# Subtracting the running maxima on TensorE in the hgt passes of a graph-network kernel

## What is computed

```
a = (kw * q_e).sum(-1) * pri[:, etype].T / sqrt(D)      # one score per edge and head
amax = segment_max(a, dst)
ea = exp(a - amax[dst])
att = ea / segment_sum(ea, dst)[dst]
h = segment_sum(m * att[:, :, None], dst)
```

## Time and profile before

| | before |
|---|---|
| median of 3 runs | 7814.15 us (7812.76 to 7823.77) |
| the profiled execution's own time | 7818.18 us |
| span of the profiled execution | 7816.4 us |
| first hgt pass, from its first load to its last add | 5353.4 to 6094.7 us |
| second hgt pass, to its last add | up to 7110.7 us |
| busy over the span | PE 66%, DVE 63%, POOL 46%, ACT 34% |

### The profile page before, as it was taken

How to read it: one execution, slowest core, us unless ns; L and a number is a source line. 1 busy time by engine, 2 the same in 40 slices (tenths; PEclk the granted TensorE clock), 3 DMA queues, 4 the chain that set the end, 5 groups by cost and what they waited for, 6 DMA issues and landing times. The chain is left out here.

```text
span 7816.4 us, 109527 instructions
## 1 busy us (share of the span) xinstructions
PE 5146.3 (66%) x21617; PEld 3624.5 (46%) x21618; DVE 4929.8 (63%) x12062; ACT 2667.4 (34%) x6461; POOL 3569.9 (46%) x3776
## 2 busy tenths in 40 slices
PE   4762667567746956676756664876777767776764
PEld 4762334334424834556733344853444444444443
DVE  6875677767766157543366665157999549996453
ACT  2551455144511210002213311224777137772321
POOL 1774677067700257760147710234666026661014
PEclk9999777777778987787856776999999899998777
DMA  2541444144411943335624411965777137772036
GB/s 83 163 145 53 116 126 125 22 120 125 125 17 49 314 121 87 88 82 212 215 78 107 106 22 31 321 192 173 211 211 208 34 124 212 210 211 72 21 98 199
DMA packets 516240, 1021.81 MB, mean 131 GB/s; under 512 B 135829, under 2 KB 276930, under 8 KB 507278
## 3 DMA queue, kind: packets, MB, share of 16 engines
q0 software_dynamic: 191360, 489.21, 23.3%
q1 hardware_dynamic: 294095, 497.29, 19.7%
q10 hardware_dynamic: 30528, 32.52, 1.2%
HBM read 928.22 MB, written 90.27 MB: 130 GB/s over the span
## 5 line engine op out<-in xcount | busy, mean ns | idle before, releaser
L731 POOL DMA_INDIRECT l_hgt_ep_g<-l_tkm,l_hgt_ep_ix x832 | 924.3, 1111 | 439.5 <-PE l_hgt_ep_out L816 235.9
L731 POOL DMA_INDIRECT l_gat_ep_g<-l_gat_th,l_gat_ep_ix x832 | 844.5, 1015 | 240.1 <-issue 232.4
L816 PE MATMUL l_gat_ep_out<-l_gat_ep_g,l_gat_ep_here 128*126 128x264 f32 x1664 | 686.0, 554 | 160.9 <-DVE l_gat_acc L965 152.4
L816 PEld LDWEIGHTS l_gat_ep_out<-l_gat_ep_g,l_gat_ep_here 128*126 128x126 f32 x1664 | 376.8, 256 | 382.5 <-DVE l_gat_acc L965 310.9
L2315 DVE TENSOR_TENSOR f_moe_experts_yb<-f_moe_experts_py,f_moe_experts_b2s 128x256 f32<-128x256 f32 x208 | 88.4, 425 | 719.3 <-PE f_moe_experts_py L2298 700.9
L2266 POOL DMA_INDIRECT f_moe_experts_xg<-f_moe_tx,f_moe_tok x208 | 196.4, 944 | 743.2 <-PE f_moe_experts_px L2279 626.8
L816 PE MATMUL l_hgt_ep_out<-l_hgt_ep_g,l_hgt_ep_here 128*126 128x288 f32 x1664 | 500.2, 424 | 53.5 <-DVE l_hgt_ep_g L951 52.2
L855 ACT COPY l_gat_ep_stage<-l_gat_ep_out 30x264 f32<-30x264 f32 x832 | 308.7, 372 | 563.2 <-PE l_gat_ep_out L816 551.5
L2486 POOL DMA_INDIRECT l_edges_g<-l_table,l_edges_ix x416 | 413.8, 995 | 179.9 <-issue 100.2
L2330 ACT ACTIVATE f_moe_experts_ht<-f_moe_experts_phid,f_moe_experts_b1b 128x128 f32<-128x128 f32 x848 | 242.0, 372 | 734.6 <-PE f_moe_experts_phid L2289 730.1
L524 POOL DMA_INDIRECT recs<-place_stage,place_pos x392 | 425.0, 1084 | 138.5 <-issue 117.4
(11 more groups left out here) (603 smaller groups left out, 11877.5 us busy)
## 6 DMA issues: line engine op xcount, KB each, us to landing
l_hgt_ep_hot<-locrow SPq DMA_DIRECT2D x208, 256.0 KB, 4.9
f_moe_experts_w1b<-in_L_ffn_w SPq DMA_DIRECT2D x32, 1024.0 KB, 6.8
f_moe_experts_w2b<-in_L_ffn_w SPq DMA_DIRECT2D x32, 1024.0 KB, 7.6
f_moe_experts_w1b<-in_L_ffn_w SPq DMA_DIRECT2D x64, 512.0 KB
f_moe_experts_w2b<-in_L_ffn_w SPq DMA_DIRECT2D x64, 512.0 KB
f_moe_experts_w1b<-in_L_ffn_W SPq DMA_DIRECT2D x56, 512.0 KB, 4.8
f_moe_experts_w2b<-in_L_ffn_W SPq DMA_DIRECT2D x56, 512.0 KB, 4.9
l_gat_ep_hot<-locrow SPq DMA_DIRECT2D x104, 256.0 KB
```

The costliest lines, as they stand in the source:

```text
L731: gp.indirect_dma_start(g[:, b % NB, j, 0:W], None, table, bass.IndirectOffsetOnAxis(ap=ix[:, b, j:j + 1].bitcast(U32), axis=0)).then_inc( ...
L816: pe.matmul(out[:, t % 4, 0:WO], here[:, b % 2, t, :], g[:, b, t, F:F + WO], start=True, stop=True).then_inc(s_out, 1)
```

## The change

In "hgt" passes alone, `x` and `less` go. TensorE's `turn_back` becomes `less_top`: a matmul of `raw` with the identity starts a sum in PSUM and a second one, of `top` with a new constant `minus` (minus the identity), adds to it, so that PSUM holds raw less maximum, in two buffers by parity of the step. ScalarE's `exponent` becomes `keep_top`: it takes the exponent straight from PSUM, and then copies the two columns of `top` to `refs`. On VectorE the backward scan follows the forward one at once, and the adds 1, 2 and 3 follow it one after the other. `scan` waits for ScalarE's copy of two steps before (`s_refs`, one more semaphore for each edge pass of any kind) in place of `s_back`, and `score` no longer waits for `s_x`. GpSimd makes `minus` at the start.

```diff
+            gp.affine_select(out=core.minus[:, :], in_=core.ones[:, :], compare_op=ALU.is_equal, fill=0.0,
+                             base=0, pattern=[[1, 128]], channel_multiplier=-1).then_inc(made, 1)
+            gp.wait_ge(made, 5)
+            gp.tensor_scalar(core.minus[:, :], core.minus[:, :], -1.0, None, ALU.mult)
...
-        x = ph.sb("x", [128, 2, CT, H])
+        x = ph.sb("x", [128, 2, CT, H]) if kind != "hgt" else None
...
+        apart = back[:, 0:2 * R].rearrange("p (b t h) -> p b t h", b=2, h=H) if kind == "hgt" else None
...
+        s_refs = ph.sem("refs")
...
+            def less_top(k, b):
+                if later(k):
+                    pe.wait_ge(s_ex, k - 1)
+                pe.matmul(back[:, b % 2 * R:b % 2 * R + R], core.ident[:, :], raw[:, b % 2, :, :].rearrange("p t h -> p (t h)"),
+                          start=True, stop=False, skip_group_check=True)
+                pe.wait_ge(s_top, k + 1)
+                pe.nop(nofuse=True)
+                pe.matmul(back[:, b % 2 * R:b % 2 * R + R], top[:, b % 2, :], core.minus[0:R, 0:R],
+                          start=False, stop=True, skip_group_check=True).then_inc(s_back, 1)
...
-                piped(pe, NCH, [(2, total(0)), (0, whose), (1, turn), (2, total(1)), (1, turn_back), (0, queries)], NB)
+                piped(pe, NCH, [(2, total(0)), (0, whose), (1, turn), (2, total(1)), (1, less_top), (0, queries)], NB)
...
+            def keep_top(k, b):
+                act.wait_ge(s_back, k + 1)
+                act.activation(g[:, b, :, X:X + H], apart[:, b % 2, :, :], ACT.Exp).then_inc(s_ex, 1)
+                act.copy(refs[:, :, bass.ds(k, 1)].rearrange("r s o -> r (s o)"), top[:, b % 2, 0:128:127]).then_inc(s_refs, 1)
...
-                piped(act, NCH, [(3, take(0)), (3, take(1)), (2, exponent), (0, one_hot), (1, rows_here)], NB)
+                piped(act, NCH, [(3, take(0)), (3, take(1)), (2, keep_top), (0, one_hot), (1, rows_here)], NB)
...
                     v.wait_ge(s_back, k - 1)
-                    v.wait_ge(s_x, k - 1)
+                    if kind != "hgt":
+                        v.wait_ge(s_x, k - 1)
...
-                    v.wait_ge(s_back, k - 1)
+                    v.wait_ge(s_refs if kind == "hgt" else s_back, k - 1)
...
-                piped(v, NCH, [now(score), add(0), now(scan), add(1), now(scan_back), add(2), now(less), add(3), now(weigh(0))], NB)
+                piped(v, NCH, [now(score), add(0), now(scan), now(scan_back), add(1), add(2), add(3), now(weigh(0))], NB)
```

More of the change, by code:

```diff
@@ L116, in constants @@
     core.low = keep.sb("low", [128, 128])
+    core.minus = keep.sb("minus", [128, 128])
     core.iota = keep.sb("iota", [128, 128])
```

## The result

The changed kernel takes 7797.32 us (median of 14 runs, 7787.74 to 7829.2), the kernel before beside it 7816.05 (14 runs, 7801.73 to 7831.4): ratio 0.9979, 95% interval 0.997 to 0.9987, 16 us less by the ratio and 19 by the medians. That is faster, as forecast, but about half of the 34 us (35 less, 1 more) that the sum had taken off. The profiled execution took 7805.18 us, span 7803.4.

A forecast was written before the change was run, and what follows sets the result against it. Two equally long chains, VectorE's queue and TensorE's loop through scans and queries, were taken to bound the step. Step 6.78 to 6.61, 0.17 x 208 = 35 us less, 1 more: 7818.2 to 7784, median 4 lower, 7780; range 7762 to 7825.

The forecast's parts named there:

- the 34 us (35 less, 1 more): Whole kernel: 0.17 x 208 = 35 us less from the steps, 1 us more for semaphores and GpSimd's constant.
- Undisturbed step 6.61: VectorE's queue in an hgt step: mean step 6.78 before, 6.61 after.
- The 0.40 that goes is paid back but for 0.03: VectorE: two instructions holding 0.40 go, but three adds standing together, each waiting for the last, take back all but 0.03.
- TensorE's loop 6.56: TensorE: queries at 4.44, next key multiplication possible 2.12 later, at 6.56, 0.05 shorter than VectorE's 6.61.
- L900 overlaps the weighing's end: VectorE, sign: the next key multiplication comes 1.14 after the weighing if nothing holds it, not 1.24 or more.
- the rival in which the gap is VectorE's own: Gap ahead of the key multiplication: steps 6.71 and 6.80, 5 us less, 7810; chance 0.22.
- The rival of free adds: VectorE: the adds' waits overlap, TensorE's loop sets the step at 6.56, 46 us less, 7769; chance 0.12.
- The rival in which it does: ScalarE late to the first add: if 0.30 late each step, step 6.91, 27 us more, 7842; chance 0.13.
- The steps' disturbances of 0.06 I leave as they are.: In the sum: steps average some 0.06 more than an undisturbed step, taken as unchanged.
- half the clock ... which the granted clock of 1.00 excludes: TensorE's four new instructions: a bound of 0.22 each, next key multiplication at 6.85, excluded by the clock.
- The two alternate, so a step takes 6.74 or some 6.83: VectorE's steps before the change: two alternating kinds, 6.74 or some 6.83, 6.78 in the middle.

The follow-up runs named there:

- scans_together: The kernel before with only VectorE's order changed, the backward scan right behind the forward one; subtraction and copy stay on VectorE: 7796.9 us, ratio 0.9987.
- pe_minus_only: The changed kernel with an add put back between the two scans: 7802.24 us, 1.0004 of the kernel before.
- after_add_last: The changed kernel with the last add moved behind the weighing, no idle matmuls: 7739.84 us, 0.991 of the kernel before.
- experiment 4: The changed kernel with the last add behind the weighing: 7739.98 us with three idle matmuls ahead of the transpose of the scores, 7739.84 with none.
- after: The changed kernel itself, first measurement and trace, against the kernel before: 7797.32 us, ratio 0.9979.
- after_second: The changed kernel measured and traced again, nothing altered, against the kernel before: 7799.53 us, ratio 0.9986.

## Why the prediction was right in direction and wrong in size

- **"Undisturbed step 6.61"**: measured 6.63. VectorE's terms, behind L923: reduction to first add 1.13, the scans 0.50, the adds 0.64 and 0.67 (forecast 0.66) with 0.21 idle, the weighing 0.38 behind the last, L923 1.13 behind that. The price that came from the earlier trace rows held. The Trainium skill's rule that operations count and semaphores don't (VectorE: DVE Perf Modes, "Rules for kernel authors") differs from this trace, which decides: these adds cost 0.64 and 0.67, not 0.37.
- **"The 0.40 that goes is paid back but for 0.03"**: right in the sum, and `scans_together` shows it stronger: 0.00. But I priced that kernel at 6.76 before it ran, as if the subtraction and the copy still cost 0.13 beside the adds. They stand inside the wait. What the change gains is the place of the backward scan alone.
- **"TensorE's loop 6.56"**: 0.18 too long. The queries start 0.31 behind the start of the second subtracting matmul (I had 0.43), and L923 can follow their start by 2.03 (`pe_minus_only`), where I used 2.12. By the step shown above that makes 4.35 + 2.03 = 6.38, and a quarter of the steps of `after_add_last` take no more than 6.40 (first pass) and 6.37 (second). It set nothing in the changed kernel, but it is why the order of experiment 4 could bring the median step down to between 6.50 and 6.55.
- **"L900 overlaps the weighing's end"**: right; the rival in which the gap is VectorE's own falls by L923 at 1.13 and by `pe_minus_only`, where the gap grows with less work on VectorE. The rival of free adds falls by the 0.21 of idle in each pair, 46.0 us in the stretch.
- **ScalarE**: the exponent from PSUM takes 0.28 (forecast 0.31) and the copy 0.19 (0.2); an estimate of 0.19 for the copy was given from the Trainium skill (ScalarE: Activation LUTs, "What ACT_TABLE_LOAD costs"), and this trace agrees with it. ScalarE did not come late to the first add in most steps: the add overlaps the reduction in 177 of 206, as in 176 before. The rival in which it does holds in a few, the three long steps at 1.00 among them, with 3.7 us over the median.
- **The step that failed** is the sentence "The steps' disturbances of 0.06 I leave as they are." Between the long steps it held: 6.70 against 6.63, a difference of 0.07. But the long steps, 7 before, became 25 (21 in the second trace), and cost some 21 (12) us more, 18 (9) of it in steps with the clock at 0.50. Over whole passes a step took 6.92 before and 6.88 after: 0.14 above the undisturbed 6.78, and 0.25 above 6.63. The sum with this term is 30 less 21 in the profiled execution, and 30 less 12 in the second, where the passes are 18.4 shorter than before. Idle matmuls, which leave the median step at 6.64, bring the passes to 31.7 us less than before (single traces) and the time to 29.5, near the 34 of the sum. That falls of the clock take the rest is shown, by the clock in the long steps and by these runs. I had read 1.00 off and used it only to exclude a price ("half the clock ... which the granted clock of 1.00 excludes"), without asking what the new order does to TensorE's idle time.
- **"The two alternate, so a step takes 6.74 or some 6.83"**: the rows that I read were two of four. For long stretches the steps of the kernel before repeat as 7.00, 6.74, 6.83, 6.74, and 47 of 206 take 7.00 to 7.05; in the changed kernel about one in four takes 6.78 instead of 6.63. So the 0.06 was no scatter but mostly one slower step of the four that `piped` unrolls. What makes that one slower stays open.

What stays open is what pattern of idle time lets the clock fall. It isn't the longest gap of a usual step (1.53 in `after_add_last`, clock up; 1.02 in the changed kernel, clock falls), nor the sum in a step (1.97 before, from three gaps; 1.62 after). What the runs do show is that the three traces with gaps of 0.60 and 1.02 around the 1.23 of the sums on these chips (`after`, `after_second`, `scans_together`) have a stretch at 0.50 in 23, 20 and 29 of 206 steps, and that filling or closing either gap brings this to 3 to 6; the kernel before has 9. Why it falls so seldom with 0.26 and 1.22 around the same sums is not settled. Nor is why TensorE releases the forward scan 0.17 late in some steps of the changed kernel and 0.23 in some of `after_add_last` and of the kernel before.

## What to carry to other kernels

Before moving small operations off a busy engine, look whether they stand inside a wait: an instruction that waits for the one just before it on its own engine pays for that openly, and work put between such a pair is free as long as it fits into the wait, so here one reordered line did all that the larger change did. A change that moves one engine's work also moves the idle gaps of the others: draw TensorE's gaps before and after, since a step that is shorter on paper can lose half its gain to falls of the clock. When two chains are about equally long, move ahead what lies on the loop between engines (here the backward scan) and behind what nobody waits for (here the last add).

## What the runs showed of the hardware

- TensorE's granted clock fell from 1.00 to 0.50, in the step shown above, behind 0.61 us of idle time, 1.23 of work and 1.02 of idle time. It stayed at 0.50 for some 3 us of unbroken work, in which four instructions of the sums took 1.88 instead of 1.15. The Trainium skill tells of a kernel with short and frequent idle times between groups of matmuls whose clock went up and down (TensorE: Matmul & The Clock Gate, "A second HAM failure mode: psum-queue depth-cycling"). The changed kernel agrees with that; the kernel before, with three short gaps a step, reads 1.00 in both stretches.
- Idle matmuls of 128 f32 columns take 0.61 for four instructions and 0.83 for six, so 0.11 for each more, as the 0.11 worked out from the earlier trace rows. They cost the kernel before no time that can be told (0.9992, 0.9983 to 1.0001).
- Two starts of adds on VectorE are 0.64 to 0.67 apart in most steps when the second waits for the first (0.75 to 0.79 in some), whether or not a subtraction of 128 x 128 and a copy of 128 x 2 stand between them.
